# Setup of an attention and experts kernel: memsets behind the weights' split, first K transfers on two queues, b2 behind the experts' first weights

## The chip, the cores and the metric

## What is computed

A gated cross attention, then a gated mixture of experts, 32 batches of 100 queries, 1444 keys, 256 features, 16 heads of 16, 12 experts, top 3:

```python
Q = layernorm(x) @ Wq.T + bq;  K = ctx @ Wk.T + bk;  V = ctx @ Wv.T + bv
attn = softmax(Q @ K.T * scale)                      # 16 heads
x = x + tanh(g_xattn) * ((attn @ V) @ Wo.T + bo)
h = layernorm(x)
probs = softmax(h @ Wr + br);  top 3 of 12, ew = softmax(top values)
out = sum over e of mask_e * w_e * (relu(h @ w1[e] + b1[e]) @ w2[e] + b2[e])
out = out * (1 - 0.8 * (phi(mean of out) > 0.7))     # phi: a small MLP on the pooled rows
x = x + tanh(g_ffn) * out
```

## The kernel before

Two stages, `attention` and `experts`, each a block with one hand-written program for each engine; the order on an engine is the order of its program, and semaphores tie the engines together.

**Attention.** Keys come in 12 tiles of up to 128 for each batch (NT = 12), in 3 chunks of 4 tiles (NC = 3). All engines run the same loop over steps g from -8 on; at step g each engine does what falls to it, and `batch_at(g, offset)` says which batch has its turn. Tile i of batch b has its V at g = 12b + i. The K of chunk j comes in two halves o: TensorE computes it and ScalarE and VectorE copy it to `k_hl` at g = 12b + 4j + 2o - 1 (L566 and L805). One step later SyncE issues eight transfers (L353, L354, four values of q, two each) that lay it out by heads in `k_stack`. The copy of the next chunk's same half waits for these (`k_stacked`). Row maxima of the scores run from g = 6 on: TensorE writes two banks `max_ps` in turn, VectorE reduces each (L641). Scores and exponentials start at g = 20, the product with V one step later (`pv_ps`).

**Its start.** SyncE issues the K and V weights, the context, x, and nine smaller weights and constants. VectorE first sets six buffers (`pv_ps`, three `q_stack`, `x_row`, `small`; L611 to L615), then splits the K and V weights into two parts (L620, L621), sets `v_ones` (L623 to L626; the weights were loaded into `v_ones[1]`, `w_kv` is its alias), copies bv (L630, L631) and enters the loop. There come the statistics of x (L821, L825), GpSimd's `inv_std` (L458, L461) and then, later in GpSimd's program, the split of the context (L446, L451), VectorE's normalisation (L830), TensorE's transpose (L996), ScalarE's copy (L530), TensorE's projection (L1003), the split of q (L555, L715). SyncE stores q to HBM (L368, four transfers), writes rows of ones into `k_stack` (L360, four), loads q as `q_stack` (L379, L381, four), and then comes the first K. ScalarE's program begins with a wait for all nine weights and the gate's tanh (L506).

**Experts.** 86 tiles of 128 rows. Twelve experts' weights are loaded in turn into `w_all`; the first twelve tiles wait for as many experts (`loaded_for`). For a tile TensorE transposes its rows (L1404), ScalarE copies them (L1279) and copies w1 and b1 of the tile's expert to `w1_c` (L1272), VectorE copies w2 to `w2_c` (L1344). TensorE multiplies by w1 (L1416), ScalarE applies the activation (L1293), TensorE multiplies by w2 (L1427), VectorE weights the result and adds b2 (L1364), GpSimd scatters it (L1213). ScalarE's program starts with the load of b2 to all partitions (L1282), then copies rows of tile 0, w1 of tiles 0 and 1, and enters the loop over tiles. VectorE multiplies b2 by the experts' weights (L1354) behind tile 0's w2.

Of the kernel before, what the change touches and what calls it, by code (L numbers as in the profile page):

```python
# [111 lines left out]
def attention(nc, x, ctxT, g_xattn, wqT, bq, wkT, bk, wvT, bv, woT, bo, wr, br,  # L112
              xs, ys, x1s, qd, table, wexp):
    with ExitStack() as ctx:
# [6 lines left out]
        def sem(name):  # L121
            return ctx.enter_context(nc.semaphore(name))
# [192 lines left out]
        def _(sp):  # L315
# [19 lines left out]
            for g in range(FIRST, LAST):  # L335
# [6 lines left out]
                for j in range(NC):  # L342
                    for o in range(KD):
                        b = batch_at(g, 4 * j + 2 * o)
                        if b is None:
                            continue

                        wait(sp, k_read, KD * (NC * b + j) + o + 1)
                        wait(sp, score_done, UH * (NT * (b - 2) + TPC * (j + 1)))
                        for q in range(4):  # L350
                            dst = k_stack[b % 2][:, 4 * o + q, k0[j]:k0[j] + CW[j]].bitcast(F32)
                            src = k_hl[32 * q:32 * q + 32, o, :, 0:CW[j]].bitcast(F32)
                            sp.dma_start(dst[0:64, :], src).then_inc(k_stacked[j][o], 16)  # L353
                            sp.dma_start(dst[64:96, :], src[:, 1, :]).then_inc(k_stacked[j][o], 16)  # L354
                if g == -1:
                    sp.wait_ge(const_ready, N_CONST)
                    for p in range(2):
                        row = k_stack[p][96:97, :, :].rearrange("p j t -> p (j t)").bitcast(F32)
                        for i in range(2):
                            sp.dma_start(row[:, ROW * ROW * i:ROW * ROW * (i + 1)],  # L360
                                         ones[0:ROW, 0:ROW]).then_inc(ones_rows, 16)
                b = batch_at(g, AT_XQ + 3)
# [8 lines left out]
                if b is not None:  # L371

                    wait(sp, q_written, 16 * 4 * (b + 1))
                    wait(sp, score_done, NT * UH * (b - 2))
                    if b == 0:
                        sp.wait_ge(stack_ready, 1)
                    for e in range(2):
                        rows, cols = slice(HD * e, HD * e + HD), slice(SQ * e, SQ * e + SQ)
                        sp.dma_start(q_stack[b % 3][2 * HD * e:2 * HD * e + 2 * HD, :, cols].bitcast(F32),  # L379
                                     qd[b % 2, rows].rearrange("d (i o) q s -> (d i) (o q) s", i=2)).then_inc(q_stacked, 16)  # L380
                        sp.dma_start(q_stack[b % 3][64 + HD * e:64 + HD * e + HD, :, cols].bitcast(F32),  # L381
                                     qd[b % 2, rows, 0:KD].rearrange("d o q s -> d (o q) s")).then_inc(q_stacked, 16)
# [121 lines left out]
        def _(act):  # L504
# [3 lines left out]
            def exps(g, u):  # L508
# [6 lines left out]
                if n >= PROBS:  # L515
                    act.wait_ge(pv_done, visit_of((n - PROBS) // UH) + 1)
                act.activation(probs[0:tw, n % PROBS, :], score_bank(n)[0:tw, 0:UH * SQ],  # L517
                               ACT.Exp, scale=SCALE).then_inc(exp_done, 1)

            for g in range(FIRST, LAST):  # L520
                b = batch_at(g, AT_POST)
# [48 lines left out]
                if b is not None:  # L570
                    wait(act, v_done, NT * b + i + 1)

                    if b == 0 and i == 0:
                        act.wait_ge(split_w, 1)
                    if b >= 2:
# [3 lines left out]
                                   ACT.Copy).then_inc(v_read, 1)  # L579
                exps(g, 3)  # L580
                b = batch_at(g, AT_POST + 6)
                if b is not None:
# [18 lines left out]
        def _(dve):  # L601
# [8 lines left out]

            dve.memset(pv_ps[:], 0.0).then_inc(setup, 1)  # L611
            for p in range(3):
                dve.memset(q_stack[p][:].bitcast(F32), 0.0).then_inc(setup, 1)
            dve.memset(x_row[:], 0.0).then_inc(setup, 1)
            dve.memset(small[:], 0.0).then_inc(setup, 1)  # L615
            own[0] += 6
            dve.wait_ge(setup, own[0])
            dve.wait_ge(kv_in, 32)
            for i in (1, 0):
                link(dve.tensor_copy(w_hi[:, i], w_kv[:, i]))  # L620
                link(dve.tensor_tensor(w_lo[:, i], w_kv[:, i], w_hi[:, i].bitcast(F32), ALU.subtract))  # L621
            for p in range(2):
                link(dve.memset(v_ones[p][:, :, :, HD:VW], 1.0))  # L623

                link(dve.memset(v_ones[p][:, NT - 1], 0.0))
                link(dve.memset(v_ones[p][0:TW[NT - 1], NT - 1, :, HD:VW], 1.0))  # L626
            dve.sem_inc(split_w, 1)
            dve.sem_inc(stack_ready, 1)
            dve.wait_ge(weights_in, 16 * N_WEIGHTS)
            link(dve.tensor_copy(bv_wide[:, 0, :], bv_c[:, 0:1].broadcast_to([128, SQ])))  # L630
            dve.tensor_copy(bv_wide[:, 1, :], bv_c[:, 1:2].broadcast_to([128, SQ])).then_inc(bias_ready, 1)  # L631

# [22 lines left out]

            for g in range(FIRST, LAST):
                maxes(g, 0)
                b = batch_at(g, AT_POST + 1)
# [237 lines left out]
        def _(pe):  # L896
# [69 lines left out]
            def times_v(g):  # L966
# [6 lines left out]
                if first == 0:  # L973

                    wait(pe, v_read, NT * (b + 1))
                    wait(pe, pv_read, b)
                for i in range(first, last + 1):
# [92 lines left out]
def experts(nc, xs, ys, x1s, table, wexp, g_ffn, w1, b1, w2, b2, wp1, bp1, wp2, bp2, out):  # L1070

    with ExitStack() as ctx:  # L1072
# [53 lines left out]
        x_in = [sem(f"x_in{p}") for p in range(AHEAD)]  # L1126
        w_in = [sem(f"w_in{e}") for e in range(NE)]
        w1_ready = sem("w1_ready")
# [40 lines left out]
        def on(t):  # L1169
            return 0 <= t < TILES  # L1170
# [5 lines left out]

        def loaded_for(eng, t):

            if t < NE:
                eng.wait_ge(w_in[t], 16 * 3)  # L1180

# [39 lines left out]
        def _(sp):  # L1221
# [9 lines left out]
            def load_weights(e):  # L1231
                sp.dma_start(w_all[:, e, 0:KD * FF].rearrange("p (k f) -> p k f", k=KD), w1[e]).then_inc(w_in[e], 16)
                sp.dma_start(w_all[:, e, KD * FF:WX], b1[e]).then_inc(w_in[e], 16)
                sp.dma_start(w_all[:, e, WX:WW].rearrange("p (m d) -> p m d", m=FM), w2[e]).then_inc(w_in[e], 16)

# [30 lines left out]
        def _(act):  # L1266
            def copy_w1(t):
                expert = act.value_load(table[0:1, bass.ds(t, 1)], min_val=0, max_val=NE - 1)

                loaded_for(act, t)  # L1270
                wait(act, h_done, FM * (t - 1))
# [3 lines left out]
            def x_copy(t):  # L1275
# [3 lines left out]
                act.activation(xT[:].rearrange("p k t -> p (k t)"), xT_ps[:], ACT.Copy).then_inc(xT_ready, 1)  # L1279

            act.wait_ge(always, 1)
            act.dma_start(b2_w[:, 0:NE, :], b2.partition_broadcast(128)).then_inc(b2_in, 16)  # L1282
            x_copy(0)
            copy_w1(0)
            copy_w1(1)
            for t in range(TILES):
# [8 lines left out]
                if on(t + 1):  # L1295
                    x_copy(t + 1)
                if on(t + 2):

                    act.wait_ge(h_relu, FM * (t + 1))
                    copy_w1(t + 2)  # L1300
# [14 lines left out]
        def _(dve):  # L1315
# [23 lines left out]
            def copy_w2(t):  # L1339
                expert = dve.value_load(table[0:1, bass.ds(t, 1)], min_val=0, max_val=NE - 1)  # L1340

                loaded_for(dve, t)
                wait(dve, y_done, t - 1)
# [145 lines left out]
```

## Time and profile before

| | us |
|---|---|
| median of 3 runs (2208.51 to 2213.41) | 2209.78 |
| profiled execution | 2204.03 |
| its span, first to last instruction | 2202.3 |
| TensorE busy in it | 2086.9 |
| VectorE busy | 1480.1 |
| ScalarE busy | 1305.6 |

Times in the trace are microseconds from the start of the span. A busy TensorE is not a TensorE at its peak, since matmuls overlap. "SPq" is SyncE's queue and "ACTq" ScalarE's: an entry there is the issue of a transfer, not its duration. The loop over g has its first step with a key tile at about 20 us; the experts begin near 1745 us.

### The profile page before, as it was taken

Reading aid. Unit: us, or ns where it says so; the run is one execution under the profiler, and the core shown is the slowest. Engines: PE = TensorE matmul, PEld = TensorE weight load, DVE = VectorE, ACT = ScalarE, POOL = GpSimd, SP = SyncE. Lnnn points to the kernel's source line nnn. Section 1 sums busy time; section 2 is a strip of 40 time slices with the busy share of each in tenths; the row PEclk is TensorE's granted clock in tenths of the full one; section 3 lists DMA queues with packets and bytes.
Section 4 is the critical chain, followed back from the end, with each engine's and each line's share of the span. In section 5 each row is a group of like instructions: output and inputs, shape, how many; then the busy total and the mean of one; then the engine's idle time right before and its main releaser. Section 6 shows DMA issues by size and latency. Waiting matters only on the chain. (4 is left out here: it accounts for less than half of the span.)

```text
span 2202.3 us, 63899 instructions
## 1 busy us (share of the span) xinstructions
PE 2086.9 (95%) x24150; PEld 1848.7 (84%) x24150; DVE 1480.1 (67%) x3330; ACT 1305.6 (59%) x3073; POOL 806.0 (37%) x1187
## 2 busy tenths in 40 slices
PE   5899999999999999999999999999998399999994
PEld 4688888888888888888888888888887299999993
DVE  4777777777777777777777777777774433333334
ACT  1366666656666656666666666666666177777771
POOL 4333344333344333443333433334431133333331
PEclk9999999999999999999999999999999699999996
DMA  5555555555555555555555555555554394333335
GB/s 137 151 132 141 142 145 135 143 137 137 138 134 140 139 141 136 137 135 135 139 139 143 140 138 140 139 137 134 136 129 149 129 313 109 59 59 58 60 52 190
DMA packets 230670, 293.42 MB, mean 133 GB/s; under 512 B 83512, under 2 KB 156188, under 8 KB 230108
## 3 DMA queue, kind: packets, MB, share of 16 engines
q1 hardware_dynamic: 204396, 258.76, 44.2%
q0 software_dynamic: 18528, 21.64, 5.2%
q10 hardware_dynamic: 7440, 8.95, 1.2%
q8 instruction: 191, 3.13, 0.6%
q14 instruction: 115, 0.94, 0.1%
HBM read 104.01 MB, written 42.92 MB: 67 GB/s over the span
## 5 line engine op out<-in xcount | busy, mean ns | idle before, releaser
L641 DVE TENSOR_REDUCE max_part<-max_ps 100x1 f32<-100x512 f32 (+1 forms) x1536 | 994.9, 655 | 353.9 <-PE max_ps L930 324.5
L517 ACT ACTIVATE probs<-score_ps 128x400 f32<-128x400 f32 x1498 | 733.4, 503 | 412.0 <-PE score_ps L913 401.5
L930 PE MATMUL max_ps<-k_stack,q_stack 96*100 96x512 f32 (+1 forms) x1536 | 597.2, 389 | 12.8 <-DVE max_part L641 12.5
L913 PE MATMUL score_ps<-q_stack,k_stack 97*128 97x200 f32 (+1 forms) x2996 | 598.3, 282 | 1.3 <-ACT probs L517 0.5
L913 PEld LDWEIGHTS score_ps<-q_stack,k_stack 97*128 97x128 f32 (+1 forms) x2996 | 463.2, 183 | 66.5 <-issue 30.4
L446 POOL TENSOR_TENSOR ctx_hi<-ctx_raw,zero_col 128x256 fp32r<-128x256 f32 (+1 forms) x384 | 213.3, 586 | 467.8 <-PE v_ps L944 430.7
L981 PE MATMUL pv_ps<-probs,v_ones 128*17 128x100 f32 x12288 | 303.1, 250 | 5.6 <-ACT pv_out L525 2.7
L981 PEld LDWEIGHTS pv_ps<-probs,v_ones 128*17 128x17 f32 x12288 | 256.0, 98 | 51.7 <-issue 37.5
L930 PEld LDWEIGHTS max_ps<-k_stack,q_stack 96*100 96x100 f32 x1536 | 257.1, 167 | 25.4 <-DVE max_part L641 20.3
L451 POOL TENSOR_TENSOR ctx_lo<-ctx_raw,ctx_hi 128x256 fp32r<-128x256 f32 (+1 forms) x384 | 257.2, 700 | 7.5
L566 ACT ACTIVATE k_hl<-k_ps,bk_c 128x512 fp32r<-128x512 f32 (+1 forms) x192 | 127.3, 663 | 215.9 <-PE k_ps L961 193.4
L1213 POOL DMA_INDIRECT results_by_token<-y_t,slot x86 | 153.9, 1789 | 258.6 <-DVE y_t L1364 242.4
L944 PE MATMUL v_ps<-w_hi,ctx_hi 128*128 128x256 f32 (+1 forms) x768 | 218.9, 285 | 10.4 <-ACT v_ones L577 10.4
L944 PE MATMUL v_ps<-w_hi,ctx_lo 128*128 128x256 f32 (+1 forms) x768 | 216.7, 282 | 0.0
L944 PE MATMUL v_ps<-w_lo,ctx_hi 128*128 128x256 f32 (+1 forms) x768 | 216.4, 282 | 0.0
L1416 PEld LDWEIGHTS h_ps<-xT,w_c 128*128 128x128 f32 x1720 | 207.4, 193 | 9.5 <-ACT w_c L1272 4.4
L1416 PE MATMUL h_ps<-xT,w_c 128*128 128x128 f32 x1720 | 208.0, 277 | 4.5 <-ACT w_c L1272 4.0
L1427 PE MATMUL y_ps<-w_c,hid 128*128 128x256 f32 x860 | 199.7, 379 | 0.0
L1293 ACT ACTIVATE hid<-h_ps,w_c 128x128 f32<-128x128 f32 x430 | 156.8, 367 | 69.2 <-PE h_ps L1416 42.1
L1364 DVE SCALAR_TENSOR_TENSOR y_t<-y_ps,wexp,b_w 128x256 f32<-128x256 f32 x86 | 41.6, 484 | 224.6 <-PE y_ps L1427 222.0
L1427 PEld LDWEIGHTS y_ps<-w_c,hid 128*128 128x128 f32 x860 | 156.8, 190 | 17.8
L577 ACT ACTIVATE v_ones<-v_ps 128x256 f32<-128x256 f32 (+1 forms) x384 | 146.6, 382 | 33.9 <-PE v_ps L944 20.2
(197 smaller groups left out, 2528.1 us busy)
## 6 DMA issues: line engine op xcount, KB each, us to landing
k_stack<-k_hl SPq DMA_DIRECT2D x512, 128.0 KB, 2.6
ctx_raw<-in_ctxT SPq DMA_DIRECT2D x64, 512.0 KB, 4.4
k_stack<-k_hl SPq DMA_DIRECT2D x512, 64.0 KB, 2.2
k_stack<-k_hl SPq DMA_DIRECT2D x256, 105.0 KB, 2.4
w_all<-in_w SPq DMA_DIRECT2D x24, 640.0 KB, 9.5
ctx_raw<-in_ctxT SPq DMA_DIRECT2D x32, 420.0 KB, 4.7
k_stack<-k_hl SPq DMA_DIRECT2D x256, 52.5 KB, 2.0
x_t<-rows_by_expert SPq DMA_DIRECT2D x86, 134.5 KB, 2.3
```

Of the source, the lines that this page charges most:

```text
L446: ins = pool.tensor_tensor(ctx_hi[:, c % 2, k, cols], ctx_raw[:, k, cols], zero[:].broadcast_to([128, CW[j] // 2]), ALU.add)
L451: ins = pool.tensor_tensor(ctx_lo[:, c % 2, k, cols], ctx_raw[:, k, cols], ctx_hi[:, c % 2, k, cols].bitcast(F32), ALU.subtract)
L517: act.activation(probs[0:tw, n % PROBS, :], score_bank(n)[0:tw, 0:UH * SQ], ACT.Exp, scale=SCALE).then_inc(exp_done, 1)
L641: dve.tensor_reduce(max_part[b % 2][:, h, j:j + 1], max_ps[m % 2][0:SQ, 0:CW[j]], AX.X, ALU.max).then_inc(max_read, 1)
L913: ins = pe.matmul(score_bank(n)[0:TW[i], 2 * SQ * p:2 * SQ * (p + 1)], k_stack[b % 2][:, 2 * u + p, 128 * i:128 * i + TW[i]], q_stack[b % ...
L930: pe.matmul(max_ps[m % 2][0:SQ, 0:CW[j]], q_stack[b % 3][0:96, h // 2, SQ * (h % 2):SQ * (h % 2) + SQ], k_stack[b % 2][0:96, h // 2, k0[j] ...
L944: ins = pe.matmul(v_ps[0:tw, 0:D], c[:, (NC * b + i // TPC) % 2, k, keys], w[:, 1, k, :], start=(k == 0 and p == 0), stop=(k == KD - 1 and ...
L981: ins = pe.matmul(pv_ps[32 * h:32 * h + VW, u * SQ:u * SQ + SQ], v_ones[b % 2][:, i, UH * u + h, :], probs[:, n % PROBS, h * SQ:h * SQ + S ...
L1213: pool.indirect_dma_start(out=ys, out_offset=bass.IndirectOffsetOnAxis(ap=slot[t % SLOTBUFS][:], axis=0), in_=y_t[t % OUT][:], in_offset=None,
L1293: act.activation(hid[t % 2][:, c, :], h_ps[c][:, 0:RT], ACT.Relu, bias=w1_c[t % 2][:, KD * FF + c:KD * FF + c + 1]).then_inc(h_relu, 1)
L1416: ins = pe.matmul(h_ps[c][:, 0:RT], w1_c[t % 2][:, k * FF + 128 * c:k * FF + 128 * c + 128], xT[:, k, :], start=(k == 0), stop=(k == KD - 1))
L1427: ins = pe.matmul(y_ps[(t - 1) % 2][:, 0:D], hid[(t - 1) % 2][:, m, :], w2_c[(t - 1) % 2][:, m, :], start=(m == 0), stop=(m == FM - 1))
```

## The change

In attention:

- VectorE: the six memsets and the `v_ones` memsets leave the place ahead of and behind the weights' split. `v_ones[0]` and `q_stack[0]` are set at g = -4, `q_stack[1]` and `v_ones[1]` at g = 5, `q_stack[2]`, `pv_ps`, `x_row` and `small` at g = 7, the copies of bv stand at g = 2. New semaphores `v_ones_set` and `pv_zero`; `stack_ready` counts to 3.
- The rows of ones are issued by ScalarE, behind its first tanh and ahead of the loop, not by SyncE at g = -1.
- For g under 20, ScalarE issues half of the eight K transfers (q = 2 and 3), behind V's copy and the exponentials of the step; SyncE issues the other half. From g = 20 SyncE issues all.

In experts:

- w1 and b1 of an expert have a semaphore of their own, w2 another; the w1 copy no longer waits for w2, nor the w2 copy for w1.
- b2's load is issued behind the copy of tile 0's w1.
- The copy of w1 of tile 1 stands behind the activations of tile 0 and the copy of tile 1's rows.

```diff
@@ attention, new helper (SyncE's eight transfers, by q)
+        def stack_keys(eng, b, j, o, some):
+            for q in some:
+                dst = k_stack[b % 2][:, 4 * o + q, k0[j]:k0[j] + CW[j]].bitcast(F32)
+                src = k_hl[32 * q:32 * q + 32, o, :, 0:CW[j]].bitcast(F32)
+                eng.dma_start(dst[0:64, :], src).then_inc(k_stacked[j][o], 16)
+                eng.dma_start(dst[64:96, :], src[:, 1, :]).then_inc(k_stacked[j][o], 16)
@@ attention, SyncE's loop
-                        for q in range(4):
...
+                        stack_keys(sp, b, j, o, (0, 1) if g < AT_SCORE else (0, 1, 2, 3))
-                if g == -1:
-                    sp.wait_ge(const_ready, N_CONST)
...
-                    if b == 0:
-                        sp.wait_ge(stack_ready, 1)
+                    if b < 3:
+                        sp.wait_ge(stack_ready, b + 1)
@@ attention, ScalarE, ahead of the loop
+            act.wait_ge(const_ready, N_CONST)
+            for p in range(2):
+                row = k_stack[p][96:97, :, :].rearrange("p j t -> p (j t)").bitcast(F32)
+                for i in range(2):
+                    act.dma_start(row[:, ROW * ROW * i:ROW * ROW * (i + 1)],
+                                  ones[0:ROW, 0:ROW]).then_inc(ones_rows, 16)
@@ attention, ScalarE's loop, V's copy
-                    if b == 0 and i == 0:
-                        act.wait_ge(split_w, 1)
+                    if b < 2 and i == 0:
+                        act.wait_ge(v_ones_set, b + 1)
...
                 exps(g, 3)
+                for j in range(NC):
+                    for o in range(KD):
+                        b = batch_at(g, 4 * j + 2 * o)
+                        if b is not None and g < AT_SCORE:
+
+                            act.wait_ge(k_read, KD * (NC * b + j) + o + 1)
+                            stack_keys(act, b, j, o, (2, 3))
@@ attention, VectorE, ahead of the loop
-            dve.memset(pv_ps[:], 0.0).then_inc(setup, 1)
-            for p in range(3):
-                dve.memset(q_stack[p][:].bitcast(F32), 0.0).then_inc(setup, 1)
-            dve.memset(x_row[:], 0.0).then_inc(setup, 1)
-            dve.memset(small[:], 0.0).then_inc(setup, 1)
-            own[0] += 6
-            dve.wait_ge(setup, own[0])
             dve.wait_ge(kv_in, 32)
...
-            for p in range(2):
+            dve.sem_inc(split_w, 1)
+
+            def set_stack(p):
+                dve.memset(q_stack[p][:].bitcast(F32), 0.0).then_inc(stack_ready, 1)
+
+            def set_ones(p):
                 link(dve.memset(v_ones[p][:, :, :, HD:VW], 1.0))
...
@@ attention, VectorE's loop
             for g in range(FIRST, LAST):
+                if g == AT_XQ + 1:
+                    set_ones(0)
+                    set_stack(0)
+                if g == CONST_SLOT - 1:
+                    dve.wait_ge(weights_in, 16 * N_WEIGHTS)
+                    link(dve.tensor_copy(bv_wide[:, 0, :], bv_c[:, 0:1].broadcast_to([128, SQ])))
+                    dve.tensor_copy(bv_wide[:, 1, :], bv_c[:, 1:2].broadcast_to([128, SQ])).then_inc(bias_ready, 1)
+                if g == CONST_SLOT + 2:
+                    set_stack(1)
+                    set_ones(1)
+                if g == CONST_SLOT + 4:
+                    set_stack(2)
+                    dve.memset(pv_ps[:], 0.0).then_inc(pv_zero, 1)
+                    link(dve.memset(x_row[:], 0.0))
+                    link(dve.memset(small[:], 0.0))
@@ attention, TensorE, product with V
                     wait(pe, v_read, NT * (b + 1))
+                    if b == 0:
+                        pe.wait_ge(pv_zero, 1)
@@ experts, SyncE
-                sp.dma_start(w_all[:, e, 0:KD * FF].rearrange("p (k f) -> p k f", k=KD), w1[e]).then_inc(w_in[e], 16)
...
+                sp.dma_start(w_all[:, e, 0:KD * FF].rearrange("p (k f) -> p k f", k=KD), w1[e]).then_inc(w1_in[e], 16)
...
@@ experts, ScalarE
-                loaded_for(act, t)
+                if t < NE:
+                    act.wait_ge(w1_in[t], 16 * 2)
...
+            x_copy(0)
+            copy_w1(0)
             act.wait_ge(always, 1)
             act.dma_start(b2_w[:, 0:NE, :], b2.partition_broadcast(128)).then_inc(b2_in, 16)
-            x_copy(0)
-            copy_w1(0)
-            copy_w1(1)
...
                 if on(t + 1):
                     x_copy(t + 1)
+                if t == 0:
+
+                    act.wait_ge(h_relu, FM)
+                    copy_w1(1)
@@ experts, VectorE
-                loaded_for(dve, t)
+                if t < NE:
+                    dve.wait_ge(w2_in[t], 16)
```

## Rows read from the trace of the kernel before

**Rows 1.** The page, parts 1 and 2: busy time, granted clock in 40 slices.

```profile
PE 2086.9 (95%) x24150; PEld 1848.7 (84%) x24150; DVE 1480.1 (67%) x3330; ACT 1305.6 (59%) x3073; POOL 806.0 (37%) x1187
...
PEclk9999999999999999999999999999999699999996
```

**Rows 2.** Timeline, 0 to 19 us: start, length, engine, line, work [idle before <- releaser].

```profile
1.00 0.48 DVE L611 MEMSET pv_ps<- 128x512 f32 x1 [1.00 <-PEq L1482]
...
1.27 0.42 SPq L322 DMA_DIRECT2D v_ones<-in_wkT  x1
...
3.48 1.39 DVE L613 MEMSET q_stack<- 97x1600 f32 x1 [0.28 <-issue]
...
6.90 0.43 DVE L620 CAST w_hi<-v_ones 128x512 fp32r<-128x512 f32 x1
...
9.48 0.22 DVE L623 MEMSET v_ones<- 128x192 f32 x1 [0.24 <-DVE w_lo L621]
...
10.25 0.20 ACT L506 ACTIVATE gate<-gate_raw 128x1 f32<-128x1 f32 x1 [8.16 <-DMA gate_raw<-in_g_xattn]
...
11.89 0.42 DVE L821 BATCH_NORM_STATS2 stats<-x_in 100x6 f32<-100x256 f32 x1
...
15.00 0.34 ACT L530 ACTIVATE xT_q<-small_ps 128x200 f32<-128x200 f32 x1 [4.54 <-PE small_ps L996]
...
15.39 2.03 PE L1003 MATMUL small_ps<-xT_q,w_qo 128*128 128x100 f32 x8 [0.43 <-ACT xT_q L530]
...
18.91 0.77 PE L961 MATMUL k_ps<-ctx_hi,w_hi 128*128 128x512 f32 x1 [1.50 <-POOL ctx_lo L451]
```

**Rows 3.** View of tile v_ones (the weights' landing place), 0 to 12 us.

```profile
DMA to landing us min/median/max: 2.9/2.9/3.0
```

**Rows 4.** Timeline, 19 to 77 us: SyncE's issues and ScalarE's copies of K.

```profile
19.97 2.59 SPq L368 DMA_DIRECT2D queries<-q_hl  x4
...
28.04 0.61 SPq L353 DMA_DIRECT2D k_stack<-k_hl  x1
...
33.17 0.62 SPq L319 DMA_DIRECT2D ctx_raw<-in_ctxT  x1
...
34.78 0.69 ACT L566 ACTIVATE k_hl<-k_ps,bk_c 128x512 fp32r<-128x512 f32 x1 [6.75 <-DMA k_stack<-k_hl]
...
41.10 0.69 ACT L566 ACTIVATE k_hl<-k_ps,bk_c 128x512 fp32r<-128x512 f32 x1 [3.25 <-PE k_ps L961]
...
46.80 0.61 ACT L566 ACTIVATE k_hl<-k_ps,bk_c 128x420 fp32r<-128x420 f32 x1 [2.27 <-PE k_ps L961]
...
66.57 0.69 ACT L566 ACTIVATE k_hl<-k_ps,bk_c 128x512 fp32r<-128x512 f32 x1 [2.50 <-PE k_ps L961]
...
76.59 0.69 ACT L566 ACTIVATE k_hl<-k_ps,bk_c 128x512 fp32r<-128x512 f32 x1 [6.07 <-DMA k_stack<-k_hl]
```

**Rows 5.** Landing of k_stack's transfers, 26 to 96 us; line 299's issues (ns).

```profile
DMA to landing us min/median/max: 2.0/2.6/4.2
...
L299 ACTq DMA_DIRECT2D rows_by_expert<-ctx_raw x6: 338/360/432, 1736.7 to 1743.1; - x6
```

**Rows 6.** Timeline, the experts' first tiles.

```profile
1755.40 0.66 PE L1404 MATMUL xT_ps<-ident,x_t 128*128 128x128 f32 x2 [20.30 <-DMA x_t<-rows_by_expert]
...
1758.69 1.28 ACT L1272 ACTIVATE w_c<-w_all 128x1285 f32 x1 [2.21 <-DMA w_all<-in_w]
...
1760.02 4.47 PE L1416 MATMUL h_ps<-xT,w_c 128*128 128x128 f32 x20 [3.96 <-ACT w_c L1272]
...
1765.29 2.47 PE L1416 MATMUL h_ps<-xT,w_c 128*128 128x128 f32 x20 [0.58 <-issue]
...
1769.98 2.39 PE L1416 MATMUL h_ps<-xT,w_c 128*128 128x128 f32 x20
```

**Rows 7.** Windows: length, PE, PEld, DVE, ACT, POOL busy, clock, DMA share, GB/s.

```profile
33.00:34.00 1.00, 0.00 (x0) 0.00 (x0) 0.00 (x0) 0.00 (x0) 0.00 (x0) 0.82 0.65 160
...
1750.00:1752.00 2.00, 0.00 (x0) 0.00 (x0) 0.00 (x0) 0.00 (x0) 0.00 (x0) 0.50 1.04 356
```

More of the change, by code:

```diff
@@ L230, in attention @@
         stack_ready = sem("stack_ready")
+        v_ones_set = sem("v_ones_set")
+        pv_zero = sem("pv_zero")
         setup = sem("setup")
@@ L349, in _ @@
                         wait(sp, score_done, UH * (NT * (b - 2) + TPC * (j + 1)))
-                        for q in range(4):
[L351 to L354, printed above, removed]
-                if g == -1:
-                    sp.wait_ge(const_ready, N_CONST)
-                    for p in range(2):
[L358 to L361, printed above, removed]
+                        stack_keys(sp, b, j, o, (0, 1) if g < AT_SCORE else (0, 1, 2, 3))
                 b = batch_at(g, AT_XQ + 3)
@@ L621, in _ @@
                 link(dve.tensor_tensor(w_lo[:, i], w_kv[:, i], w_hi[:, i].bitcast(F32), ALU.subtract))
-            for p in range(2):
+            dve.sem_inc(split_w, 1)
+            def set_stack(p):
+                dve.memset(q_stack[p][:].bitcast(F32), 0.0).then_inc(stack_ready, 1)
+            def set_ones(p):
                 link(dve.memset(v_ones[p][:, :, :, HD:VW], 1.0))
@@ L626, in _ @@
                 link(dve.memset(v_ones[p][0:TW[NT - 1], NT - 1, :, HD:VW], 1.0))
[L627 to L631, printed above, removed]
+                dve.sem_inc(v_ones_set, 1)
             n_chain = [0]
@@ L1126, in experts @@
         x_in = [sem(f"x_in{p}") for p in range(AHEAD)]
-        w_in = [sem(f"w_in{e}") for e in range(NE)]
+        w1_in = [sem(f"w1_in{e}") for e in range(NE)]
+        w2_in = [sem(f"w2_in{e}") for e in range(NE)]
         w1_ready = sem("w1_ready")
@@ L1175, in stored_by @@
                 eng.wait_ge(y_stored[t % OUT], 16 * (t // OUT + 1))
-        def loaded_for(eng, t):
-            if t < NE:
-                eng.wait_ge(w_in[t], 16 * 3)
         block = ctx.enter_context(nc.Block())
@@ L1231, in load_weights @@
             def load_weights(e):
-                sp.dma_start(w_all[:, e, 0:KD * FF].rearrange("p (k f) -> p k f", k=KD), w1[e]).then_inc(w_in[e], 16)
-                sp.dma_start(w_all[:, e, KD * FF:WX], b1[e]).then_inc(w_in[e], 16)
-                sp.dma_start(w_all[:, e, WX:WW].rearrange("p (m d) -> p m d", m=FM), w2[e]).then_inc(w_in[e], 16)
+                sp.dma_start(w_all[:, e, 0:KD * FF].rearrange("p (k f) -> p k f", k=KD), w1[e]).then_inc(w1_in[e], 16)
+                sp.dma_start(w_all[:, e, KD * FF:WX], b1[e]).then_inc(w1_in[e], 16)
+                sp.dma_start(w_all[:, e, WX:WW].rearrange("p (m d) -> p m d", m=FM), w2[e]).then_inc(w2_in[e], 16)
             for t in range(AHEAD - 1):
```

## The prediction

> **What bounds the kernel now.** I read the page first. TensorE is busy for 2086.9 us of a span of 2202.3 us; the granted clock dips in three places, the first slice, the change of stage (about 1745 us) and the end [rows 1]. In between there is little to win for an edit that moves setup work only. The change touches the first two places, so the question is how much earlier the full part of each stage begins; what follows slides forward by that amount.
>
> I write g for a step of the attention loop. ScalarE's copy of K stands at odd g, so its instances are milestones: g = 3 at 34.78, 5 at 41.10, 7 at 46.80, 13 at 66.57, 15 at 76.59 us [rows 4]. Their usual distance is 6.6 us for two g (66.57 less 46.80, three pairs). Two of them stand out, as they waited for a K transfer: 6.75 us idle at g = 3 and 6.07 us at g = 15. SyncE issues the eight transfers of a K half 0.64 us apart (28.04 to 33.17 us) while one lands 2.6 us after its issue [rows 4, 5]: there the issuing queue is the bound, not the transfer. From g = 7 on the copies wait for TensorE, which trades the two maxima banks with VectorE; a faster queue doesn't shorten that.
>
> **Start, up to the first K.** Ahead of the weights' split the six memsets leave, 1.00 to 6.90 us. The V and K weights were issued by 1.27 us and land 3.0 us later, at 4.3 us [rows 2, 3]. The split took from 6.90 to 9.48 less a wait of 0.24, so 2.3 us, and now ends at 6.7. The v_ones memsets and the bias copies (9.48 to 11.89, 2.4 us) leave too [rows 2]. The statistics of x start when x has landed, which no row shows: it lies between 4.3 us (the weights, issued before it) and 10.25 us (all weights, issued behind it). As much again as the first two weights (512 KB of context) stands ahead of x, so I take 7.5, the middle. From the statistics (11.89) to ScalarE's copy of the transposed x (15.00) is 3.1 us, so this could be at 10.6.
>
> But ScalarE stands elsewhere. It waits for all weights until 10.25 us and then issues the four transfers of ones: 4 x 0.64, to 13.1. The copy of x moves from 15.00 to 13.1, gain 1.9. TensorE's queue projections take 2.03 us behind it; then K's first matmul waited for GpSimd's split of the context until 18.91 [rows 2]. That split hangs on the same statistics, 4.4 us earlier now, so it is done near 14.4, and K's matmuls start behind the projections at 15.5: gain 3.4. (x may land 1.1 us later than I take without a cost; at 10.25 the gain would be 1.7.) VectorE's first q_stack and v_ones memsets (1.67 and about 1.0: 2.7 us) run from 10 to 12.7 beside these waits; without that cover they cost at most 2.7.
>
> **SyncE.** In order: four stores of queries from 19.97 us, four ones, four q_stack, K at 28.04 [rows 4]. The ones leave, but they hid the landing of the queries (2.4 us, by the 2.6 of [rows 5]), for which q_stack waits. So queries from 16.8 to 19.4, wait to 22.0, q_stack to 24.6, K at 24.7: gain 3.4 and not 3.4 + 2.7. Then four issues instead of eight: to 27.2, landed 29.8. ScalarE's four go out from 20 us and are down long before. The copy at g = 3 runs at 29.8 for 34.78, **gain 5.0**. At g = 4 ScalarE issues its half from about 32.4 to 35.0 and only then copies K for g = 5, against 41.10: **gain 6.1**. The q_stack and v_ones memsets of g = 5 (2.7 us, 33 to 35.7) lie beside that; I cost them at 0, at most 2.7.
>
> **Memsets at g = 7.** The six took 5.90 us; less two q_stack of 1.39 + 0.28 this is 2.56, and with the waits between x_row and small 2.8 [rows 2]. VectorE reduces maxima by then and TensorE has two banks only, so they are on the path: **loss 2.8**, bounds 0 and 3.3.
>
> **The second stall.** At g = 10 to 12 SyncE has queries, their landing and q_stack on top of K. With four issues for a K its K of g = 12 is down 15.2 us after g = 10 began (2.6 + 2.6 + 2.3 + 2.6 + 2.6 + 2.5), and the copy at g = 15 needs it at 5 x 3.3 = 16.4. The stall goes: 76.59 less 66.57 is 10.0 against 6.5, **gain 3.5**, bounds 0 and 3.5. What is late next is the trade of maxima banks. ScalarE pays 2.6 us of issuing each two g, where it waited 2.3 to 2.5 us for TensorE ahead of its K copies [rows 4]; the 0.3 left lie beside VectorE's reductions. From g = 20 all is as before.
>
> Attention: 6.1 - 2.8 + 3.5 = **6.8 us** (bounds 1.7 and 9.6).
>
> A rule speaks against the two queues. By the Trainium skill (DMA: Bandwidth & Descriptors, Issuing engines are not separate DMA queues) starting transfers from several engines saves only the time of the sequencer, usually small beside the transfer. The trace agrees with the first half; 5.1 us of issuing against 2.6 us of landing is not small. By the rule's second half only the start would stay, 3.4 - 2.8 = 0.6 us in this stage.
>
> **Experts.** b2 goes first (12 x 256 values to 128 partitions, 1.57 MB), tile 0's rows are there at 1755.40, TensorE starts at 1760.02 behind the copy of w1 (1758.69, 1.28 us) [rows 6]. At the 0.356 MB/us of this stretch [rows 7] b2 is 4.4 us, so the rows land at 1751.0; w1, 0.66 MB later, at about 1753; TensorE starts at 1754.4, 5.6 us earlier. It doesn't keep that. b2 goes out at 1753.3, in the middle of the weights: until w1 of tile 1 is down, rows, weights and b2 are 3.8 MB, from 1750.4 at 0.37: 1760.7. Tile 1's copy, now behind tile 0's activations and the copy of x (1760.0), ends at 1762.2; tile 1 starts at 1762.3 for 1765.29, 3.0 left. TensorE's gap after tile 0 (4.47 us at 1.2 GHz, to 1758.9) is now 3.4 us. In the idle stretch from 31.4 us the granted clock was down for part of 33 to 34 us (0.82) [rows 7]; before, tile 1 had the full clock and took 2.47 us [rows 6]. At 1.2 GHz it takes 4.5, and tile 2 begins near 1769.2 for 1769.98: 0.8 left. With the clock kept, 2.2 are left: w1 of tile 2 is not down before 1764.5, and its copy stands ahead of tile 1's activations. From tile 2 on TensorE has no gap and the lead stays. b2's product on VectorE moves to about 1760 to 1764, ahead of tile 0's result at 1767. I take **1.2**, near the cold end, bounds -1 and 5.6.
>
> **Sum.** 6.8 + 1.2 = 8.0 us. The profiled execution took 2204.03 us (its span 2202.3), 5.75 under the median of the runs, 2209.78. It becomes 2196.0; the median 2201.8.
>
> **Rivals.** (A) The forecast, 5 to 10.5 us less: 0.52.
> (B) Covers fail: the memsets at g = 5 count as well and the stall at g = 15 stays, since SyncE's burst has 1.2 us to spare: 6.1 - 2.8 - 2.7 + 1.2 = 1.8, 2208.0. For it: that spare is small. Against: SyncE sheds half of its K work. 0.22.
> (C) More: the memsets at g = 7 fall beside a wait of TensorE, and the experts keep 4: 6.1 + 3.5 + 4 = 13.6, 2196.2. For it: tile 0 alone gains 5.6. Against: b2's bytes have to pass before tile 2 in any order. 0.16.
 For it: those were 1.3 us apart, not back to back. 0.08. The Trainium skill (Perfetto Trace Analysis, DMA Instruction - HWDGE (DVE, Sync)) draws a wait for a lock ahead of a generator that two sequencers share; it doesn't name ScalarE's, and no row here shows such a wait.
> (E) The change moves nothing that ends last, within 2 us: 0.02.
>
> A measurement of this kernel tells about 0.2%, 4.4 us, from no change. Faster: A, C and 0.02 of B, 0.70. Within: the rest of B and E, 0.22. Slower: D, 0.08. The range holds A, nearly all of B and the lower half of C's outcomes: 2195 to 2209.
>
> **What would show it.** The split at 4.3; ScalarE's copy of x at 13.1 with the ones right ahead; SyncE's first K at 24.7; K's copies at 29.8 (g = 3), 35.0 (g = 5), about 43.5 (g = 7), then 6.5 us apart without a wait for a transfer at g = 15; in the experts tile 0 starts 5.6 us sooner after the stage's start, tile 1 runs at the lower clock. Issues over 1.1 us on ScalarE would be D. Time lost in the 1600 us between, where nothing is edited, would prove the forecast wrong.

## The result

| | before | changed |
|---|---|---|
| median of 6 runs | 2211.05 us | 2202.81 us |
| profiled execution | 2204.03 us | 2202.73 us |
| its span | 2202.3 us | 2201.0 us |

The medians differ by 8.2 us (forecast: 8.0 less). The ratio is 0.9958, with a 95% interval of 0.9946 to 0.9971; that is 9.3 us less, 6.4 to 11.9. The two profiled executions differ by 1.3 us only, since that of before was 7 us under the median of its runs. A single pair of traces is a poor witness for the total here; its first steps are a good one.

The timeline of the changed kernel, its start, with the lines that answer to [rows 2] and [rows 4]:

```profile
4.23 0.43 DVE L625 CAST w_hi<-v_ones 128x512 fp32r<-128x512 f32 x1 [4.23 <-DMA v_ones<-in_wkT]
...
7.43 0.43 DVE L842 BATCH_NORM_STATS2 stats<-x_in 100x6 f32<-100x256 f32 x1 [0.86 <-DMA x_in<-in_x]
...
12.93 0.34 ACT L535 ACTIVATE xT_q<-small_ps 128x200 f32<-128x200 f32 x1 [3.04 <-issue]
13.32 2.03 PE L1026 MATMUL small_ps<-xT_q,w_qo 128*128 128x100 f32 x8 [2.80 <-ACT xT_q L535]
15.05 0.77 PE L982 MATMUL k_ps<-ctx_hi,w_hi 128*128 128x512 f32 x1
...
16.58 2.59 SPq L366 DMA_DIRECT2D queries<-q_hl  x4
20.63 0.59 SPq L377 DMA_DIRECT2D q_stack<-queries  x1
...
23.21 0.72 SPq L295 DMA_DIRECT2D k_stack<-k_hl  x1
...
28.32 0.69 ACT L571 ACTIVATE k_hl<-k_ps,bk_c 128x512 fp32r<-128x512 f32 x1 [3.71 <-DMA k_stack<-k_hl]
...
33.47 0.69 ACT L571 ACTIVATE k_hl<-k_ps,bk_c 128x512 fp32r<-128x512 f32 x1 [2.75 <-DMA k_stack<-k_hl]
...
39.16 0.61 ACT L571 ACTIVATE k_hl<-k_ps,bk_c 128x420 fp32r<-128x420 f32 x1 [2.26 <-PE k_ps L982]
...
50.56 0.61 ACT L571 ACTIVATE k_hl<-k_ps,bk_c 128x420 fp32r<-128x420 f32 x1 [1.26 <-PE k_ps L982]
...
71.72 0.69 ACT L571 ACTIVATE k_hl<-k_ps,bk_c 128x512 fp32r<-128x512 f32 x1 [4.12 <-issue]
```

The weights' split starts when the weights land and the copy of x when ScalarE has issued the ones ("issue": it waited for nothing else). SyncE's first K stands at 23.2 us, K's copies at 28.3 (g = 3), 33.5 (5), 39.2 (7), 50.6 (9) and 71.7 (15), against 34.8, 41.1, 46.8, 53.5 and 76.6 before. The lead is 6.5, 7.6, 7.6, 2.9 and 4.9 us: something between g = 7 and 9 takes 4.7 of it.

VectorE and TensorE there, same kernel, timeline:

```profile
38.18 1.39 DVE L630 MEMSET q_stack<- 97x1600 f32 x1 [0.28 <-issue]
...
39.68 0.48 DVE L675 MEMSET pv_ps<- 128x512 f32 x1
40.21 0.28 DVE L676 MEMSET x_row<- 100x269 f32 x1
40.56 0.07 DVE L677 MEMSET small<- 100x16 f32 x1
...
41.41 0.47 PE L951 MATMUL max_ps<-k_stack,q_stack 96*100 96x512 f32 x1 [2.29 <-DVE max_part L647]
```

and the windows behind it (columns as in [rows 7]):

```profile
40.00:41.00 1.00, 0.00 (x0) 0.00 (x0) 0.85 (x4) 0.00 (x0) 0.00 (x0) 1.00 1.07 389
...
42.00:43.00 1.00, 1.00 (x7) 0.81 (x6) 0.97 (x2) 0.41 (x2) 0.61 (x2) 0.61 0.89 219
43.00:44.00 1.00, 1.00 (x5) 0.83 (x4) 1.00 (x3) 0.31 (x1) 1.00 (x3) 0.50 0.13 31
...
48.00:49.00 1.00, 1.00 (x6) 0.90 (x5) 0.51 (x1) 0.27 (x2) 0.00 (x0) 0.50 0.50 114
49.00:50.00 1.00, 1.00 (x7) 0.94 (x6) 0.78 (x2) 0.30 (x2) 0.00 (x0) 0.97 0.90 153
```

TensorE waits 2.29 us for the maxima that stand behind the four memsets. Behind this hole its granted clock is 0.50 from before 43 up to 49 us, so in this trace a part of the loss is at the lower clock, after the hole. The other traces differ in this. att_only has a hole of 2.18 us and the lower clock behind it for some 3 us. after_again has a hole of 2.16 us and full clock behind it; there the clock had been low ahead of the memsets:

```profile
36.00:37.00 1.00, 1.00 (x5) 0.65 (x5) 0.91 (x3) 0.00 (x0) 1.00 (x3) 0.50 0.02 8
...
44.00:45.00 1.00, 0.99 (x7) 0.69 (x6) 1.00 (x2) 0.72 (x2) 0.68 (x2) 1.00 0.16 37
```

So was it in att_only2 (0.50 from 37 to 40 us), where TensorE came late to the maxima and waited 0.62 us only, and in both_best, which has no memsets at g = 7. So the clock can dip here without the memsets too.

The experts' first tiles, timeline of the changed kernel, for [rows 6]:

```profile
1747.02 0.38 SPq L1249 DMA_DIRECT2D x_t<-rows_by_expert  x1
...
1753.12 4.64 PE L1441 MATMUL h_ps<-xT,w_c 128*128 128x128 f32 x20 [3.17 <-ACT w_c L1293]
...
1761.01 1.28 ACT L1293 ACTIVATE w_c<-w_all 128x1285 f32 x1 [2.40 <-DMA w_all<-in_b]
...
1762.34 4.21 PE L1441 MATMUL h_ps<-xT,w_c 128*128 128x128 f32 x20 [4.15 <-ACT w_c L1293]
...
1768.76 2.39 PE L1441 MATMUL h_ps<-xT,w_c 128*128 128x128 f32 x20
```

I count from the first transfer of rows in the stage: before it stood at 1748.50 us, and tiles 0, 1 and 2 began 11.5, 16.8 and 21.5 us behind it. Changed they begin 6.1, 15.3 and 21.7 us behind it: tile 0 wins 5.4 us and tile 2 none. TensorE idles 4.15 us ahead of tile 1, waiting for its w1 and b1, and tile 1 takes 4.21 us for 2.47.

### The profile page after: what moved, and what is told of

Same layout as the page of the kernel before. It is cut to its first block and busy times, and to the rows that moved or that the text cites. A ratio compares the mean times of both kernels' runs of the same rounds, so it can differ in the third digit from the quotient of the medians.

```text
span 2201.0 us, 63903 instructions
## 1 busy us (share of the span) xinstructions
PE 2091.8 (95%) x24150; PEld 1852.5 (84%) x24150; DVE 1483.3 (67%) x3330; ACT 1306.5 (59%) x3073; POOL 805.9 (37%) x1187
## 5 line engine op out<-in xcount | busy, mean ns | idle before, releaser
L934 PEld LDWEIGHTS score_ps<-q_stack,k_stack 97*128 97x128 f32 (+1 forms) x2996 | 462.8, 183 | 69.9 <-issue 30.4
```

The source lines that it names most:

```text
L934: ins = pe.matmul(score_bank(n)[0:TW[i], 2 * SQ * p:2 * SQ * (p + 1)], k_stack[b % 2][:, 2 * u + p, 128 * i:128 * i + TW[i]], q_stack[b % ...
```

## The experiments

The kernels were timed in three groups, each beside the kernel before on one chip: before_again to exp_only, memsets_only to exp_late, and the last four. Before's medians there were 2194.0, 2208.79 and 2210.05 us; only ratios are compared between groups. The comparison of the result section is called the first group, these the second, third and fourth. Microseconds in the table are one less the ratio, times before's median.

| kernel | ratio | 95% interval | us less |
|---|---|---|---|
| before_again | 1.0001 | 0.9992 to 1.0010 | 0 |
| after_again | 0.9964 | 0.9952 to 0.9976 | 7.9 |
| att_only | 0.9963 | 0.9951 to 0.9976 | 8.1 |
| exp_only | 0.9999 | 0.9990 to 1.0008 | 0.2 |
| memsets_only | 0.9988 | 0.9977 to 0.9999 | 2.7 |
| queues_only | 0.9969 | 0.9955 to 0.9983 | 6.8 |
| att_early | 0.9962 | 0.9947 to 0.9976 | 8.4 |
| exp_late | 0.9993 | 0.9983 to 1.0003 | 1.5 |
| att_only2 | 0.9962 | 0.9947 to 0.9976 | 8.4 |
| att_early2 | 0.9956 | 0.9943 to 0.9969 | 9.7 |
| exp_order | 0.9985 | 0.9977 to 0.9994 | 3.3 |
| both_best | 0.9942 | 0.9929 to 0.9955 | 12.8 |

**Twins: how far does one trace stray?** Both kernels with no edit.

> The kernel before, unchanged, as its own twin: it shows how far one execution strays from the next with nothing edited. Theory: ratio 1.000 within 0.0015; K's copy of g = 3 again at 34.8 us and of g = 15 at 76.6 (the start is the same each time), but the 30 batches between drift by some microseconds from one profiled execution to the next, as single stalls of about 1 us come and go. Rival: the batches take the same time in every execution, and the lead of 4.9 us at 150 us that shrank to 1.2 us at 1718 us was eaten by the change itself.

> The changed kernel, unchanged. Theory: 8 us less than before again (ratio 0.9945 to 0.997), with the start's milestones as in its first profile (K's copies at 28.3, 33.5, 39.2, 71.7 us) and another drift in the middle. Rival (the change eats its lead in the middle): the drift is again against it, the profiled end no more than 2 us under that of before.

The times repeat: 1.0001, and 0.9964 for the 0.9958 of the first comparison. In before_again K's copies stand at 34.77 (g = 3) and 76.89 us (g = 15), 0.0 and 0.3 us from [rows 4]. In after_again they stand at 28.61, 34.77, 41.31 and 70.30: 1.3 us later than the first trace at g = 5, and 1.4 us earlier at g = 15. ScalarE's copy of `pv_out` for batch 30 comes 6.0 us earlier in after_again than in before_again (1675.87 for 1681.87), not 1.3 as in the first pair. So the first pair's small difference was largely the draw of its executions.

Why g = 15 came later in the first trace, timeline of after, ScalarE's issues and the copy behind them:

```profile
67.22 0.58 ACTq L295 DMA_DIRECT2D k_stack<-k_hl  x1
...
67.83 0.87 ACTq L296 DMA_DIRECT2D k_stack<-k_hl  x1
...
68.73 0.62 ACTq L295 DMA_DIRECT2D k_stack<-k_hl  x1
69.38 2.23 ACTq L296 DMA_DIRECT2D k_stack<-k_hl  x1
```

and of after_again:

```profile
67.41 0.57 ACTq L295 DMA_DIRECT2D k_stack<-k_hl  x1
68.02 0.88 ACTq L296 DMA_DIRECT2D k_stack<-k_hl  x1
68.93 0.62 ACTq L295 DMA_DIRECT2D k_stack<-k_hl  x1
69.58 0.62 ACTq L296 DMA_DIRECT2D k_stack<-k_hl  x1
70.30 0.69 ACT L571 ACTIVATE k_hl<-k_ps,bk_c 128x512 fp32r<-128x512 f32 x1 [2.51 <-PE k_ps L982]
```

One issue took 2.23 us instead of 0.62, and ScalarE, which issues and copies in one order, was 1.6 us late at once (idle 4.12 us for 2.51). Long issues are not new with the second queue: in before, where ScalarE issues no K, SyncE's issue at 72.42 us took 1.25 us, in the burst that the copy at g = 15 waits for, and one at 48.56 took 1.53. New is that such an issue can now hold up ScalarE's own work.

**One half of the change alone.** att_only has attention as changed and `experts` as before; exp_only has it the other way round (the diff of the change cut at `def experts`).

> The attention part of the change alone, the experts as before. Theory from the two traces: the start gains 4.9 us and the experts' part nothing (tile 2 starts 21.48 us after the stage's first transfer before and 21.74 after), so this should reach nearly all of the change: 4 to 8 us under before. Rival, the forecast's split of 6.8 and 1.2: the same within 1.2. A second rival: the experts' edit carries half of it, and this gives 3 to 4 us.

> The experts' part alone, attention as before. Theory: tile 0 starts 5.1 us earlier after the first transfer of the stage, tile 1 waits 2.4 us for b1 and runs at the lower clock, tile 2 has lost it all: within 0.5 us of before. Forecast: 1.2 less. Rival: 3 to 4 us less, if in most executions the clock is kept over the gap.

Attention alone is the whole change, as far as the times can tell: 8.1 us for 7.9 in the same group, each within 2.8. The experts' part is 0.2 us, between 2.2 us less and 1.8 us more. In exp_only's trace the clock did not hold over the gap:

```profile
1735.60 0.38 SPq L1226 DMA_DIRECT2D x_t<-rows_by_expert  x1
...
1742.74 4.43 PE L1418 MATMUL h_ps<-xT,w_c 128*128 128x128 f32 x20 [3.34 <-ACT w_c L1270]
...
1752.14 4.64 PE L1418 MATMUL h_ps<-xT,w_c 128*128 128x128 f32 x20 [4.75 <-ACT w_c L1270]
...
1759.20 2.39 PE L1418 MATMUL h_ps<-xT,w_c 128*128 128x128 f32 x20
```

Tile 2 begins 23.6 us behind the first transfer here, 20.1 in after_again (1732.39 to 1752.48) and 21.7 in after; with the old experts it is 21.5 (before, att_only2), 21.6 (both att_early), 21.8 (memsets_only), 22.0 (queues_only), 22.7 (att_only) and 22.9 (before_again). The means are 21.8 with the new experts and 21.9 with the old.

**Memsets or queues?** Experts as before in both. memsets_only leaves the ones and K on SyncE:

```diff
-                        stack_keys(sp, b, j, o, (0, 1) if g < AT_SCORE else (0, 1, 2, 3))
+                        stack_keys(sp, b, j, o, (0, 1, 2, 3))
...
-                            stack_keys(act, b, j, o, (2, 3))
```

queues_only puts ScalarE's ones and its half of K (the same lines) into the kernel before.

> Attention's memsets and bias copies moved as in the change; the ones and all K transfers stay on SyncE; experts as before. Forecast's terms: x's chain is no longer behind the ones on ScalarE (copy of x at 10.6 to 13), K's first matmul at 14.4 to 15.5 us, SyncE's first K at about 24 to 25, so 3.4 us or a little more from the start; the waits for K transfers at g = 3 and g = 15 stay, and the memsets of g = 5 and 7 fall into VectorE's stream. If the wait at g = 15 absorbs the memsets of g = 7: 3.4 us less than before. If not: 3.4 - 2.8 = 0.6 less. Rival, the memsets carry the change: 7 to 8 less.

> The ones and half of the early K transfers on ScalarE's queue, the memsets where they were, experts as before. Forecast's terms: the first K at 28.0 us less the ones (2.7) plus the bared wait for the queries (2.3), so about the same; K's copy of g = 3 at 28 + 2.6 + 2.6 = 33, of g = 5 about 3 us earlier than 41.1, the wait at g = 15 gone (3.5): 5 to 6.5 us less than before in all. Rival by the page's rule (issue time is small): within 1 us of before. Rival, shared generator: slower.

memsets_only gains 2.7 us (0.2 to 5.1), queues_only 6.8 (3.8 to 9.9). The traces show why the memsets carry little by themselves. In memsets_only the first copy of K is 4.3 us ahead (17.53 for 21.85), but at g = 3 the lead is 3.8 (30.94, behind a wait of 7.77 us for a K transfer), at g = 9 it is 1.0 (52.48), at g = 15 2.4. In queues_only the start is where it was, and the queue makes 2.5 us at g = 3 (32.24), 4.2 at g = 5 (36.91) and 7.1 at g = 15. (The ones moved with it: SyncE's first K stands at 27.07 us for 28.04. No kernel parts the two.)

```profile
69.49 0.69 ACT L569 ACTIVATE k_hl<-k_ps,bk_c 128x512 fp32r<-128x512 f32 x1 [2.77 <-PE k_ps L971]
```

for the 76.59 with 6.07 us of waiting of [rows 4]. Both queues issued back to back, timeline of queues_only:

```profile
28.09 0.57 ACTq L293 DMA_DIRECT2D k_stack<-k_hl  x1
...
28.43 0.61 SPq L293 DMA_DIRECT2D k_stack<-k_hl  x1
...
28.70 0.65 ACTq L294 DMA_DIRECT2D k_stack<-k_hl  x1
...
29.08 0.59 SPq L294 DMA_DIRECT2D k_stack<-k_hl  x1
```

Each of these issues takes 0.57 to 0.65 us with the other queue at work, as 0.6 alone. I had named issues over 1.1 us on ScalarE as the sign of rival D. Of the 40 K issues that start on ScalarE's queue between 23 and 81 us in this trace one is over it (1.14), and in after one (2.23); the usual one stays near 0.6, and single long ones are there with one queue too. So the two queues did not slow each other in the way that D needs. The Trainium skill (DMA: Bandwidth & Descriptors, Issuing engines are not separate DMA queues) says that issuing is usually small beside the transfer. By that rule queues_only would be within 1 us of before. This case doesn't agree: 6.8 us timed and 7.1 at g = 15.

**The memsets of g = 7 ahead of the split.** att_early and att_early2 are att_only with this edit (and the semaphores' counts to match):

```diff
+            dve.memset(q_stack[2][:].bitcast(F32), 0.0).then_inc(setup, 1)
+            dve.memset(pv_ps[:], 0.0).then_inc(setup, 1)
+            dve.memset(x_row[:], 0.0).then_inc(setup, 1)
+            dve.memset(small[:], 0.0).then_inc(setup, 1)
+            own[0] += 4
+            dve.wait_ge(setup, own[0])
             dve.wait_ge(kv_in, 32)
...
-                if g == CONST_SLOT + 4:
-                    set_stack(2)
-                    dve.memset(pv_ps[:], 0.0).then_inc(pv_zero, 1)
-                    link(dve.memset(x_row[:], 0.0))
-                    link(dve.memset(small[:], 0.0))
```

> The attention part of the change with the four memsets of g = 7 (third q_stack, pv_ps, x_row, small) put back ahead of the weights' split, where VectorE waits for the weights until 4.2 us anyway; experts as before. In the first trace of the changed kernel they cost 2.3 us of TensorE idle and the lower clock from 42.6 to 49 us, together 4.7 us of lead. Theory: 3 to 5 us less than attention's part alone (12 under before). Rival: what follows at g = 8 to 15 is bound by transfers or the two banks in a way that gives the time back anyway: within 1 us of attention's part alone.

> The attention part of the change alone, again, on the chip of the next three runs, so that they can be compared with it: 7 to 8 us under before. Theory: at batch 0's product (its copy out of the bank) it is 5 to 8 us ahead of before, with K's copy of g = 9 at 49 to 50.6 us, late by TensorE's gap behind the memsets of g = 7 and the lower clock after it.

> Attention's part with the four memsets of g = 7 ahead of the weights' split, again, beside attention's part alone. Its trace had batch 0's product 11.7 us ahead of before, 4.7 us more than the mean of the changed kernels, but its timed gain was 0.38% against 0.37%. Theory: 3 to 5 us less than attention's part alone on the same chip. Rival: the 4 us of lead are given back in the middle, in the batches that have their place in time by something else; then both kernels take the same within 1.5 us.

VectorE has set all four by 3.6 us and waits for the weights still (timeline of att_early):

```profile
3.48 0.07 DVE L626 MEMSET small<- 100x16 f32 x1
4.24 0.43 DVE L631 CAST w_hi<-v_ones 128x512 fp32r<-128x512 f32 x1 [0.68 <-DMA v_ones<-in_wkT]
```

From K's copy at g = 5 to that at g = 9 it takes 12.6 and 12.8 us (33.49 to 46.12, 33.42 to 46.23), as before the change (12.4), where the four traces with the memsets at g = 7 take 17.1, 15.6, 15.4 and 14.9. both_best, below, has the memsets ahead too and takes 13.7 (34.74 to 48.42), with the lower clock from 37 to 40 us. The four traces are 2.7 us slower in the mean than these three, the first of them 4.4 slower than the two of att_early. The timed gain is 9.7 us against 8.4 in the fourth group, where the medians are even the same (2199.18 and 2199.14), and 8.4 against att_only's 8.1 across the second and third. The intervals overlap: about 3 us are shown at g = 9, in the time they are not. The traces of the fourth group show them given back: ScalarE's copy of `pv_out` for batch 0 stands at 132.26 us in att_early2 and 134.43 in att_only2, that for batch 30 at 1681.57 and 1681.61. That is the rival of the last expectation.

**b2 later.** exp_late and exp_order have attention as before. exp_late issues b2 behind tile 1's copy of w1, and VectorE does tile 1's places and w2 ahead of its wait for b2. Its ScalarE edit, against the changed kernel:

```diff
             copy_w1(0)
-            act.wait_ge(always, 1)
-            act.dma_start(b2_w[:, 0:NE, :], b2.partition_broadcast(128)).then_inc(b2_in, 16)
...
                     copy_w1(1)
+                    act.wait_ge(always, 1)
+                    act.dma_start(b2_w[:, 0:NE, :], b2.partition_broadcast(128)).then_inc(b2_in, 16)
```

exp_order does the same with both copies first, `copy_w1(0)`, `copy_w1(1)`, b2, and nothing between tile 0's activations and tile 1.

> Attention as before; the experts as changed, but b2's load issued behind tile 1's copy of w1, and VectorE's places and w2 copy of tile 1 ahead of its wait for b2. Theory: b2's 1.57 MB between the weights of tiles 0 and 1 is what took the lead of tile 0 back; without it tile 1's w1 is down in time, TensorE's gap ahead of tile 1 is about 2 us in place of 4.1 and the clock holds, tile 2 starts 18 to 19 us after the stage's first transfer in place of 21.5 to 23.6: 3 us less than before. Rival: the bytes have to pass at some time, and tile 3 or 4 waits for them instead: within 1 us of before.

> Attention as before. Experts: w1 of tile 0 and of tile 1 are copied one after the other ahead of tile 0's activations, as in before; b2's load is issued behind both; VectorE takes places and w2 of tile 1 ahead of its wait for b2. Theory: with b2 moved alone the gap ahead of tile 1 stays (2.0 us) and tile 1 runs at the lower clock for 4.64 us; without the gap (0.6 us, as before) tile 1 takes 2.47 us, and tile 2 starts 17 us after the stage's first transfer in place of 21.3 to 21.5: 3 to 5 us less than before. Rival, bytes or VectorE (b2's product of 3.36 us ahead of tile 0's result) take it back at tile 2 or 3: within 1 us.

exp_late: 0.9993, not told from nothing. Its gap ahead of tile 1 did shrink, to 2.03 us, but tile 1 still ran at the lower clock and tile 2 began 21.3 us behind the first transfer:

```profile
1763.17 4.64 PE L1420 MATMUL h_ps<-xT,w_c 128*128 128x128 f32 x20 [2.03 <-ACT w_c L1270]
```

exp_order: 3.3 us less (1.3 to 5.1), tile 2 at 19.1 us:

```profile
1751.00 0.38 SPq L1226 DMA_DIRECT2D x_t<-rows_by_expert  x1
...
1757.10 4.07 PE L1417 MATMUL h_ps<-xT,w_c 128*128 128x128 f32 x20 [3.21 <-ACT w_c L1270]
...
1763.81 4.10 PE L1417 MATMUL h_ps<-xT,w_c 128*128 128x128 f32 x20 [2.43 <-ACT xT L1277]
...
1770.12 2.39 PE L1417 MATMUL h_ps<-xT,w_c 128*128 128x128 f32 x20
```

The gain is in my range, its mechanism is not the one I wrote down. The gap of 0.6 us that I expected is 2.4 us, since tile 1's w1 is down only at 1760.9 and holds up tile 0's activations, and tile 1 took 4.10 us. What is won is the start of tile 1, 12.8 us behind the first transfer for 16.8 in before and 15.3 in after.

**Both.**

> The two variants together: the four memsets ahead of the split, and the experts with both w1 copies first and b2 behind. Theory, if both give what their traces promise: 12 + 4 = 16 us less than before (0.993). If the lead is given back in the middle: 8 + 4 = 12. If b2's bytes decide: 8 to 12.

12.8 us less than before (9.9 to 15.7), the fastest of all; after_again had 7.9 in another group and att_only2 8.4 (5.3 to 11.7) in this one. These intervals overlap, so how much more it gains than the change is not settled. Its tile 2 begins 19.0 us behind the first transfer (1743.92 to 1762.91). The sum of att_early2 and exp_order, 13.0, is what it gives.

## Why the forecast was right, step by step

For these means I take the five traces with the old attention (before, before_again, exp_only, exp_late, exp_order) and the four with the new one (after, after_again, att_only, att_only2).

| step | forecast | measured |
|---|---|---|
| weights' split starts | 4.3 us | 4.23 |
| statistics of x | 7.5 | 7.43 |
| ScalarE's copy of x, behind the ones | 13.1 | 12.93 |
| K's first matmul | 15.5 | 15.05 |
| SyncE's first K | 24.7 | 23.21 |
| lead at g = 5 | 6.1 us | 7.1 (41.05 for 33.9) |
| memsets at g = 7 | -2.8 | g = 5 to 9: -3.4 (15.75 us for 12.39); of this the memsets 2.7 (13.04 with them ahead) |
| second stall | +3.5 | +2.9 (20.2 us for 23.2, g = 9 to 15) |
| lead at g = 15 | 6.8 | 6.7 (76.6 for 69.9) |
| experts | +1.2 | 0.2 timed (-1.8 to 2.2) |

The rows up to SyncE's first K are of after alone.

**The start** was right in its order: the ones on ScalarE, and not x's own chain, set the copy of x. memsets_only bears this out, with the ones on SyncE the copy stands at 10.67 us, and I had put it at 10.6. Two of the agreements are partly luck. 7.5 was the middle of two bounds and not read from a row. The 13.1 had two misses of opposite sign: the gate's tanh ran at 9.68 us for 10.25, and the four issues of ones took 3.19 us for 2.6. SyncE's first K came 1.5 us sooner than I had it, most of it from the wait for the queries: q_stack went out 1.46 us after their last issue ended (16.58 + 2.59 to 20.63), where I had put 2.6. ScalarE issued its half of g = 4 from 30.34 us on (its second transfer stands at 30.96) where I had 32.4, and this makes the lead at g = 5 larger.

**The memsets at g = 7** were on the path as forecast, in size too: 2.7 us for 2.8. But this agreement hides a term that I put at nothing, TensorE's clock. It stood at 0.50 for 3 to 6 us in all four traces, twice ahead of the memsets and twice behind them. From g = 5 to 9 it takes 3.4 us more than with the old attention, above my bound of 3.3, and both_best, with the lower clock and no memsets there, takes 0.9 to 1.1 us more than att_early and att_early2. The memsets at g = 5 cost nothing that shows: from g = 3 to 5 it takes 4.64 and 4.74 us in the two att_early traces, which have them, and 4.67 in queues_only, which has not; behind them VectorE still waited for ScalarE's copy in all four traces (0.28 to 1.58 us).

**The second stall** is gone in three of four traces. The reason I gave, that SyncE's K for g = 12 lands in time, is right (ScalarE waits for TensorE, 2.51 us, as in the steady part). What I had not seen is that ScalarE's own slow issue can put 1.6 us there. I had put another 0.3 us of ScalarE's issuing beside VectorE's reductions, at no cost. From g = 9 to 13 it takes 13.37 us in the mean for 13.08, so about that much is seen; no kernel shows what makes it.

**The experts'** 1.2 us can't be told from the timed 0.2, whose interval holds it, but one step behind it failed in the traces. Tile 0's gain of 5.6 was 5.4, tile 1 ran at the lower clock, as I had taken for the likelier case, and I had 0.8 left at tile 2 from this; the traces have it between 1.4 us better and 2.1 worse than [rows 6]. The time went into tile 1's b1 and w1, which were there for the copy 14.0 us behind the first transfer in after where I had 12.2; tile 1 began at 15.3 for 13.8. My sum had 3.8 MB ahead of them. The window of after from 1747 to 1761 us shows 337 GB/s for 14 us, 4.7 MB, so some of the later weights, issued meanwhile, passed ahead of them. exp_only's copy began at 15.2 and after_again's at 11.7, the latter without a wait for the weights; what makes them differ is open.

**What the forecast excluded happened a little.** I had said that time lost in the 1600 us between would prove it wrong. From batch 0's to batch 30's copy of `pv_out` it takes, group by group:

| group | old attention | new attention | variants |
|---|---|---|---|
| first | 1544.7 | 1548.3 | |
| second | 1536.5, 1536.3 | 1539.4, 1537.3 | |
| third | 1545.6 | | memsets_only 1546.7, queues_only 1550.0, att_early 1549.5 |
| fourth | 1544.4 | 1547.2 | att_early2 1549.3, both_best 1548.0 |

No line of the loop is edited there, and each kernel with an edit in attention needs 1 to 5 us more. The granted clock of that stretch is 1.00 in every trace, so it is not the clock. TensorE's waits from 160 to 1650 us show about the same sum, here those of after and below them before's:

```profile
PE max_ps L951 <- DVE max_part L647: 6.4, 13, 0.9
PE score_ps L934 <- ACT probs L515: 3.3, 5, 0.8
```

```profile
PE max_ps L930 <- DVE max_part L641: 6.2, 14, 0.6
PE score_ps L913 <- ACT probs L517: 0.5, 1, 0.5
```

9.7 us against 6.7, where the stretch is 3.6 us longer; queues_only 9.7 and att_early 10.1 against 6.2 of exp_late in their group. They are single waits of under 1 us, spread over the batches. Why there is more of them in the changed kernels is open: no kernel here was made to tell it. The lead at batch 0's copy is 7.9 us (144.1 for 136.2); at batch 30 it is 1.3 in the first group, 6.2 in the second and 7.8 in the fourth. So 8.0 forecast and 7.9 to 9.3 timed agree in part because two misses, 1.1 us more lead out of batch 0 and the loss behind it, have opposite signs. The profiled execution, which I had put at 2196.0 us, took 2202.73: I moved one execution by the whole lead, and single executions stray by as much.

**Rivals.** D, the shared generator, is out by queues_only's issues and its time. Neither half of B happened: the memsets at g = 5 were covered, and SyncE's K for g = 12 came in time; the 1.6 us at g = 15 in one trace are ScalarE's own issue. C was not reached by the change. both_best makes 12.8 us of C's 13.6 by other edits: the four memsets in VectorE's wait for the weights, and b2 behind both copies of w1.

## What to carry to other kernels

Compare the time of issuing a burst with the time of landing. Here eight issues took 5.1 us for a landing of 2.6, and a second queue was worth 6.8 us even though its engine had other work, since that engine waited for TensorE just then. Setup work that fills no wait of its own engine doesn't get cheaper by moving it later: look for the engine's wait for its first load (here 3.2 us of VectorE, 1.0 to 4.2) before putting it into a loop where another engine trades buffers with it. In these traces that gave 2 to 3 us at the start of the loop, but no gain that the times can show, so follow a lead to the end before you count it. A load taken from the head of a queue has to go somewhere; ask which wait its bytes stand ahead of next, and whether the gap they make costs the clock too.

## What the runs showed that was not expected

- A hole of 2.3 us in TensorE's work was followed by 6 us at half clock (0.50 from 43 to 49 us in after), one of 2.16 us in after_again by none. Ahead of the experts' tile 1 the six traces with gaps of 2.0 to 4.75 us have it at 4.10 to 4.64 us, the eight with gaps of 0.5 to 1.3 at 2.47 to 2.50, though tile 0 ran at 4.07 to 4.64 in all of them.
- The issue of one K transfer took 2.23 us for the usual 0.62, with nothing on ScalarE ahead of it but three like it; why is open.
- Profiled executions of kernels with the same attention program differ at batch 0's end by 2.3 us with the old one (143.0 to 145.4) and by 4.0 with the new (134.4 to 138.5), and the profiled execution of before was 7 us under the median of its runs: a lead of 8 us can look like 1.3 us in one pair of traces.
